# Trees layer of a fused decoder: second rows of a sequence first, then first rows of the next, on four engines and in the gather queue

## The reference

```python
logits = x @ W_in.T + b_in
act = gelu(logits)
act4 = act.reshape(B, P, G, FAN)            # P = 4 trees, FAN = 4, G nodes in a tree
decisions = argmax(act4, axis=-1)
for d in range(DEPTH):
    ...                                     # current = the child that decisions names
masked = act4 * mask[..., None]             # only nodes on the path count
new_logits = masked.reshape(B, HID) @ W_out.T
```

## Time and profile before

| what | us |
| --- | --- |
| median of three runs | 2393.78 |
| lowest and highest | 2384.61, 2397.09 |
| the profiled execution, its own time | 2402.84 |
| its span in the trace | 2401.0 |
| trees layer: from the first statistics to its last instruction | 740 to 1131 |
| PE busy over the span | 1728.6 |
| DVE busy | 1223.4 |
| ACT busy | 868.5 |
| POOL busy | 497.1 |
| gathers, line 2154, 128 of them | 133.1, and 329.4 of idle time before them |

### The profile page before, as it was taken

How to read it: one execution, slowest core, us unless ns; L and a number is a source line. 1 busy time by engine, 2 the same in 40 slices (tenths; PEclk the granted TensorE clock), 3 DMA queues, 4 the chain that set the end, 5 groups by cost and what they waited for, 6 DMA issues and landing times. The chain is left out here.

```text
span 2401.0 us, 34756 instructions
## 1 busy us (share of the span) xinstructions
PE 1728.6 (72%) x11928; PEld 1187.7 (49%) x11952; DVE 1223.4 (51%) x4294; ACT 868.5 (36%) x1799; POOL 497.1 (21%) x637
## 2 busy tenths in 40 slices
PE   3228745767887887865649979986775556799978
PEld 1107614334543676755424446663444444577756
DVE  5754534235525777854246633335553555666532
ACT  1132233424452375745215544332443220133322
POOL 0000000012100434341043200003202331555311
PEclk8665568558997899986769988986887785799979
DMA  2000000021100656572042100002101000000000
GB/s 80 0 9 1 0 7 19 0 79 45 45 2 6 209 176 222 181 261 85 0 132 65 48 11 1 0 24 69 43 21 52 0 1 0 1 2 3 2 1 18
DMA packets 79740, 115.43 MB, mean 48 GB/s; under 512 B 8416, under 2 KB 60384, under 8 KB 78816
## 3 DMA queue, kind: packets, MB, share of 16 engines
q0 software_dynamic: 18432, 67.38, 8.2%
q1 hardware_dynamic: 58560, 44.87, 6.7%
q10 hardware_dynamic: 2592, 1.18, 0.2%
HBM read 88.82 MB, written 1.05 MB: 37 GB/s over the span
## 5 line engine op out<-in xcount | busy, mean ns | idle before, releaser
L2154 POOL DMA_INDIRECT f_rows<-tree_table,f_index x128 | 133.1, 1040 | 329.4 <-DVE f_index L2210 142.4
L2367 PE MATMUL f_ps_o<-f_rows,shared_sb 128*128 128x128 f32 x1024 | 133.4, 294 | 55.1 <-ACT f_rows L2439 54.1
L1307 ACT ACTIVATE x_probs<-x_ps_z 128x768 f32<-128x768 f32 (+1 forms) x128 | 117.4, 917 | 130.7 <-PE x_ps_z L1172 72.1
L2367 PEld LDWEIGHTS f_ps_o<-f_rows,shared_sb 128*128 128x128 f32 x1024 | 128.6, 208 | 61.2 <-ACT f_rows L2439 56.9
L2439 ACT ACTIVATE f_rows<-f_rows,f_low_act 128x128 f32<-128x128 f32 x512 | 153.0, 387 | 0.8
L2249 DVE CUSTOM_DVE_ANT_0 f_rows<-f_rows,f_xn 128x128 f32<-128x128 f32 x512 | 111.9, 287 | 53.5 <-DMA f_rows<-tree_table,f_index 50.7
L1015 DVE TENSOR_REDUCE x_minus_max<-x_ps_s 128x4 f32<-128x1024 f32 x64 | 78.1, 1224 | 69.3 <-PE x_ps_s L1172 69.1
L1163 PE MATMUL x_ps_z<-x_queries,x_keys 64*128 64x256 bf16 (+1 forms) x512 | 47.8, 266 | 47.4 <-DMA x_queries<-x_max_pieces 28.7
L1632 PE MATMUL f_ps_h<-f_xnT,weights 128*128 128x512 f32 x144 | 77.4, 666 | 2.3 <-ACT f_hT L1697 2.3
L1307 ACT ACTIVATE a_probs<-a_ps_z 128x768 f32<-128x768 f32 x64 | 51.9, 811 | 68.8 <-PE a_ps_z L1169 68.8
L1644 PEld LDWEIGHTS f_ps_y<-weights,f_hT 128*128 128x128 f32 x576 | 69.7, 191 | 14.3 <-issue 12.6
(11 more groups left out here) (623 smaller groups left out, 4395.7 us busy)
## 6 DMA issues: line engine op xcount, KB each, us to landing
x_queries<-x_pieces SPq DMA_DIRECT2D x96, 64.0 KB, 2.1
x_keys<-x_pieces SPq DMA_DIRECT2D x84, 64.0 KB, 2.1
a_queries<-a_pieces SPq DMA_DIRECT2D x48, 64.0 KB, 2.1
weights<-w_L_ffn SPq DMA_DIRECT2D x1, 2985.5 KB, 9.9
a_keys<-a_pieces SPq DMA_DIRECT2D x42, 64.0 KB, 2.0
weights<-w_L_ffn SPq DMA_DIRECT2D x1, 2449.0 KB, 10.0
weights<-w_L_ffn SPq DMA_DIRECT2D x1, 2176.0 KB, 9.5
f_rows<-tree_table,f_index POOLq DMA_INDIRECT x128
```

The costliest lines, as they stand in the source:

```text
L1307: a.activation(probs[:, r % HELD, :, :], ps_z[:, :, 0:WIDE], ACT.Exp, scale=scale).then_inc(exped, 1)
L2154: pool.indirect_dma_start(rows[:, u % 2, j, tree, :], None, g.tree_table, bass.IndirectOffsetOnAxis(index[:, u % 2, low, j * TREES + tree: ...
L2367: last = pe.matmul(ps_o[:, low, j, :], g.ident, rows[:, u % 2, j, tree, OUT + f * D:OUT + (f + 1) * D], start=k == 0, stop=k == TREES * FA ...
```

## The change

The diff reorders the steps and the gathers; each engine issues the same instructions as before.

```diff
         order_at = {}
         for h in STEPS:
-            for low, u in ((0, h), (1, h - 1)):
+            for low, u in ((1, h - 1), (0, h)):
                 for j in range(HALVES):
...
             for h in range(UNITS):
-                gather(1, h)
                 if 2 <= h + 1 < UNITS:
                     gather(0, h + 1)
+                gather(1, h)
...
         # vector engine, step h
                 if ahead:
                     prepare(h + 3)
+                if before:
+                    dots(1, h - 1, 0)
+                if h >= 2:
+                    finish(h - 2)
+                if before:
+                    dots(1, h - 1, 1)
+                    add_low(0, h - 1)
                 if here_now:
                     dots(0, h, 0)
-                if before:
-                    add_low(0, h - 1)
-                if here_now:
                     dots(0, h, 1)
-                if h >= 2:
-                    finish(h - 2)
-                if here_now:
                     go_down(h, 0)
-                if before:
-                    dots(1, h - 1, 0)
-                if here_now:
                     go_down(h, 1)
-                if before:
-                    dots(1, h - 1, 1)
```

More of the change, by code:

```diff
@@ L2389, in _ @@
                     sum_dense(h + 1, 0)
-                if here_now:
-                    sum_low(0, h, 0)
+                if before:
+                    sum_low(1, h - 1, 0)
                 if next_too:
@@ L2395, in _ @@
                     project(h + 3, 0)
+                if before:
+                    sum_low(1, h - 1, 1)
+                if here_now:
+                    sum_low(0, h, 0)
+                if ahead:
+                    project(h + 3, 1)
                 if here_now:
                     sum_low(0, h, 1)
[L2398 to L2403, removed]
         @block.scalar
@@ L2454, in _ @@
                     take_masked(h + 1, 0)
[L2455 to L2458, removed]
+                if before:
+                    gelu_low(1, h - 1, 0)
+                    scale_rows(1, h - 1, 0)
                 if next_too:
@@ L2462, in _ @@
                     take_xT(h + 3)
+                if before:
+                    gelu_low(1, h - 1, 1)
+                if here_now:
+                    gelu_low(0, h, 0)
+                if before:
+                    scale_rows(1, h - 1, 1)
+                if here_now:
+                    gelu_low(0, h, 1)
+                    scale_rows(0, h, 0)
+                if ahead:
+                    activate(h + 3, 0)
                 if here_now:
                     scale_rows(0, h, 1)
[L2465 to L2472, removed]
                 if ahead:
```

## The result

The changed kernel took 2420.49 us (median of 4 runs, 2415.22 to 2423.97), beside 2395.44 us for the kernel before on the same chip. The ratio is 1.0109 (95% interval 1.0069 to 1.0149), so it is about 25 us slower, with 16.5 at the lower end of the interval. A later repetition on another chip gave 2410.86 us and a ratio of 1.0075 (1.0046 to 1.0104), 18 us slower. The forecast of 2406 had the right sign and too small a size; both medians lie inside the range.

A forecast was written before the change was run, and what follows sets the result against it. The prediction took a loop of waits among POOL's gathers, DVE, ACT and PE to bound the trees layer. A later head, four 41.8 us steps and the tail gave +12.3 us, 2406 on the median; range 2389 to 2424.

The forecast's parts named there:

- The loop of the changed kernel: Trees layer's round trip through PE's sums, POOL's gathers and DVE's dots: full steps of 41.8 us, against 41.5 before.
- The slow sum: PE's first sum of second rows, after 6 us idle: 5.5 us taken, bounds 3.8 or slow beyond that sum.
- Rival B: PE's slow clock spreads to dense sum, projection and next sum: 4.5 us more per step, 2424; chance 0.14.
- The slow gather: One POOL gather per step, beside DVE's large multiply, takes 2.69 us instead of 0.94: 1.8 added, bounds 0 and 1.8.
- Head: Start of the layer: dense sum and projection precede the first sum, moving g(1,0,0) from 822.45 to 830.5.
- Tail: Last steps of the layer: second-half dots at 1091.1 and 1128.0, end at 1143.1 against 1130.8 before.
- The sum: All terms of the trees layer together: +12.3 us, nothing after the stage touched, 2406 on the median.
- the later first round trip: Layer's start: first gather of second rows goes out later; named as one of two things lost.
- the idle PE in every step: PE waits 6 us for scaled second rows in each step; named as one of two things lost.
- A: Rival: ACT and PE set the floor if the sum is fast or no gather slow; 2394 to 2399, chance 0.28.
- C: Rival: DVE sets the pace, steps of 35.5 us, if g(1,h,0) ends on POOL by t + 30; 2377, chance 0.10.

The follow-up runs named there:

- e6: The changed kernel with the descent's large DVE multiply issued as four pieces of 128x512 instead of one of 128x2048; 2408.69 us, ratio 1.0058.
- e1: The changed kernel, but PE and ACT work step 0's first rows at once, as in the kernel before; 2404.19 us, ratio 1.0037.
- r_after: The changed kernel run once more, unchanged, on another chip; 2410.86 us, ratio 1.0075.
- e5: The kernel before with only POOL's queue changed, first rows of the next sequence ahead of second rows; 2380.45 us, ratio 0.9936.
- e8: e7 with the projections on PE and activate on ACT also moved, behind the sums and second-row scales; 2373.20 us, ratio 0.9893.
- e7: The kernel before with only POOL's queue in the changed order, plus the large multiply in four pieces; 2384.22 us, ratio 0.9943.
- e9: e8 with the large multiply whole again; 2421.84 us, ratio 1.0067.

## Why the prediction was right, and where its size was off

- **The loop of the changed kernel.** Right, nearly to the row, up to step 6. Steps of 41.8 were forecast; the dots of second rows began at 840.78, 882.69, 924.31, 966.18 and 1009.18, steps of 41.9, 41.6, 41.9 and 43.0, mean 42.1. POOL idled 15.4 and 5.2 us ahead of the two halves of first rows (15 and 5 forecast) and not ahead of second rows, until the last sequence (26.88 us at 1114.34). Dots of first rows never waited for a gather; dots of second rows waited 3.9, 6.4, 6.2, 5.0, 8.0 and 4.1 us in steps 1 to 6 (6 forecast), and 18.7 and 18.3 in steps 7 and 8.
- **The slow sum.** 5.5 was taken from one row of two. Seven of seven were slow, 6.05 on average (5.48 to 6.68); the steps came out 0.3 us longer than forecast. Rival B's slow projections did not come: 2.55 right behind the slow sum.
- **The slow gather.** 1.8 was taken; 1.89 to 2.91 less 0.94 is 1.0 to 2.0. Right, and e6 shows its cause.
- **Head.** The term, +8, was right (8.9 by e1, 7.8 by the fastest heads). Its place was not: g(1,0,0) was forecast at 830.5 and came at 828.69, which looks right to 2 us and is two errors against each other. The layer began 5.0 us later in that execution (first matmul at 749.65 against 744.63), and its head was 7.2 us shorter than forecast (44.4 against 43.6 + 8.0), since the prologue's projections were fast.
- **Tail.** Second rows of unit 6 were forecast at 1091.1 for the second half and came at 1092.31; the last at 1128.0, came at 1129.64; the end at 1143.1, came at 1143.96.
- **The sum.** +12.3 was forecast, +12.4 is the difference of the two profiled spans, and this agreement is luck too. The layer itself grew by 8.1 us between these two profiles (386.2 to 394.3), and it began 5.0 us later in the second. The weak step is the baseline: the sum was made against one execution of before, and carried over to the median as it was. That execution had the slowest head that its code shows. Against the fastest head (35.5) the same change is 7.8 to 8.9 in the head and 8.1 in the body (350.1 less 342.0), 16 to 17 us, where 18 (r_after) and 25 were timed. The prediction even noted that the profiled execution stood 9 us over the median, and did not ask which rows of the stage held it.
- **What is lost.** The prediction named the later first round trip, which is right, and the idle PE in every step, which is not: the repetitions of the kernel before have the same idle stretch and the same slow sums, and steps as long. The other half of the loss is the last round trip. The prediction's own sum has it (57.1 us from the start of step 7 to the end, where the profile of before has 53.0; 56.8 came), but its words do not.
- **The rest.** Of the 25 us of the first timing some 8 lie outside what any trace of the layer shows; the repetition's 18 do not need them, and the first interval reaches down to 16.5. This stays open.
- **Rivals.** A (floor of ACT and PE) fell on the slow sums, as its condition said. B was argued against with a step that was the shorter of two in spite of its slow sum; that was step 5, which has no projection, so it showed nothing. C was set low for the right reason: the last gather of g(1,h,0) ended on POOL at t + 36.5 (959.85 + 0.94 against 924.31), as forecast, where C needed t + 30. What the prediction overlooked is that the queue's order alone would be a gain (e5); it costed only both parts together.

## What to carry to other kernels

When a change has several edits, cost them one by one: here the queue's edit alone gave 0.6%, and the edit of the engines' order turned it into a loss. In a loop over sequences, cost the first and the last round trip by themselves: the steps between kept their length, and the loss stood at the two ends, where no other sequence fills a longer wait. A stage in which the matmul engine often waits can vary by several microseconds between executions of the same code, here by 8; take two profiles before a sum is made against one. And ahead of a release (here PE's sums, which free buffers for gathers) it pays to have nothing that is wanted later than the release: moving the projections behind the sums took 11 us off in the timed runs (e8 against e7).

## What the runs showed of the hardware

- The same 6 matmuls take 2.55 or 4.10 us, and the granted clock over the same stretch is 0.67, 0.87 or 1.00, in executions of the same code. After waits of 7.2 to 8.5 us the next 32 matmuls took 5.5 to 6.7 us, in all five cases of the changed kernel's profile, and 3.84 us after waits of up to 3.0 there.
- A gather's issue on POOL takes 0.94 us alone and 1.9 to 3.0 if it begins early in a DVE multiply of 128x2048; it then ends 0.8 us after the multiply. Beside the same multiply in four pieces it takes 1.43 at most.
- One kernel, e9, had PE and DVE stop without a named releaser while gathers ran, mostly for 0.6 to 1.3 us at a time and once for 6.1; its neighbour e8, with three more DVE instructions in a descent, had none of it. The cost, 43 us of DVE's time in the layer, is larger than any effect of order tried here.
